# Attention phase: each pair's substitution starts ten operations earlier, and its result is stored ahead of the masked product

## What is computed

```
P = where(strict, (k*beta) @ k.T * L, 0)          # per head and chunk, 64 x 64
Ainv = inverse by powers of P;  v = Ainv @ v;  k_cumdecay = Ainv @ (k*beta*exp(g))
step over chunks:  attn = where(tril, q @ k.T * L, 0);  v_new = v_i - kcd_i @ S
                   o_i = (q*exp(g)) @ S + attn @ v_new
                   S   = S*exp(g_last) + (k*exp(g_last-g)).T @ v_new
o = rmsnorm(o) * silu(gate);   x = x + o @ Wo
```

## Time and profile before

| what | value |
|---|---|
| median of 3 runs | 1290.39 us (1282.06 to 1291.25) |
| profiled execution | 1290.93 us, span 1288.8 us |
| TensorE busy over the span | 1040.7 us (81%) |
| VectorE busy over the span | 937.1 us (73%) |
| ScalarE busy over the span | 605.8 us (47%) |
| GpSimd busy over the span | 399.1 us (31%) |
| substitution, L1772 and L1769 | 416 + 416 operations, 152.4 + 149.6 us busy on VectorE |
| product with the inverse, L1422 | 2048 matmuls, 101.7 us busy, 69.2 us of waits before them |
| first and last substitution in the trace | 265 and 855 us from the span's start |

### The profile page before, as it was taken

One profiled execution on the slowest core, in us unless ns is written; L12 is line 12 of the kernel. 1 busy time (PEld: TensorE's weight loads), 2 busy tenths in 40 slices (PEclk: granted clock), 3 DMA queues, 4 the chain that ended last, 5 costly groups with the idle time before them and its releaser, 6 DMA issues. The chain is left out here.

```text
span 1288.8 us, 38550 instructions
## 1 busy us (share of the span) xinstructions
PE 1040.7 (81%) x15510; PEld 757.8 (59%) x15510; DVE 937.1 (73%) x2432; ACT 605.8 (47%) x1614; POOL 399.1 (31%) x580
## 2 busy tenths in 40 slices
PE   3999977766887877887878786567999979699968
PEld 2888844434555554555555555445888867245546
DVE  3877645378777888877887877752777638699966
ACT  2343254434666666665666754455433245110134
POOL 3666520210211211211211211112666538520027
PEclk9999988977988889988988987776999979799969
DMA  9000022334334344334334334310000004866003
GB/s 259 1 1 1 1 100 75 87 75 100 66 90 97 82 77 100 70 86 99 80 78 102 84 74 85 76 36 6 1 1 1 1 21 98 204 160 187 2 3 129
DMA packets 282626, 93.32 MB, mean 72 GB/s; under 512 B 208976, under 2 KB 275408, under 8 KB 282448
## 3 DMA queue, kind: packets, MB, share of 16 engines
q1 hardware_dynamic: 247056, 84.03, 27.4%
q10 hardware_dynamic: 35392, 6.82, 2.8%
HBM read 56.20 MB, written 30.41 MB: 67 GB/s over the span
## 5 line engine op out<-in xcount | busy, mean ns | idle before, releaser
L1772 DVE TENSOR_TENSOR delta_tmp<-delta_PR 128x130 f32<-128x130 f32 (+12 forms) x416 | 152.4, 366 | 11.3
L1769 DVE TENSOR_TENSOR delta_PR<-delta_PR,delta_tmp 128x130 f32<-128x130 f32 (+12 forms) x416 | 149.6, 360 | 11.9
L1422 PE MATMUL psum<-delta_T,delta_pad 128*32 128x128 f32 x2048 | 101.7, 381 | 69.2 <-DMA delta_T<-inverse_scratch 68.6
L1422 PEld LDWEIGHTS psum<-delta_T,delta_pad 128*32 128x32 f32 x2048 | 86.2, 157 | 82.7 <-DMA delta_T<-inverse_scratch 75.5
L1873 POOL TENSOR_TENSOR delta_E<-delta_S,both_egl 128x128 f32<-128x128 f32 x32 | 13.5, 423 | 352.8 <-PE psum L1406 337.1
L1621 ACT ACTIVATE delta_y<-psum 32x128 f32<-32x128 f32 x256 | 68.5, 267 | 89.2 <-PE psum L1456 44.7
L506 POOL TENSOR_TENSOR ffn_H<-ffn_hid,ffn_H 128x512 fp32r<-128x512 f32 x48 | 61.6, 1289 | 59.2 <-DVE ffn_H L472 59.2
L1637 ACT ACTIVATE delta_wide<-delta_S 32x128 f32<-32x128 f32 x256 | 78.2, 306 | 3.2
L506 POOL TENSOR_TENSOR first_H<-first_hid,first_H 128x512 fp32r<-128x512 f32 x48 | 61.6, 1290 | 53.3 <-DVE first_H L472 53.3
L1469 PEld LDWEIGHTS psum<-delta_y,delta_Kd 32*32 32x32 f32 x2048 | 23.6, 113 | 91.5 <-ACT delta_y L1621 90.0
L1406 PE MATMUL psum<-delta_MV,delta_KT 32*32 32x128 f32 x2048 | 66.4, 280 | 10.6 <-ACT delta_E L1571 10.6
(11 more groups left out here) (278 smaller groups left out, 2587.0 us busy)
## 6 DMA issues: line engine op xcount, KB each, us to landing
within_scratch<-delta_PT SPq DMA_DIRECT2D x128, 64.0 KB, 2.1
delta_PR<-within_scratch SPq DMA_DIRECT2D x16, 512.0 KB, 4.3
inverse_scratch<-delta_PR SPq DMA_DIRECT2D x16, 512.0 KB, 3.1
space_T<-taps_scratch SPq DMA_DIRECT2D x8, 1024.0 KB, 6.1
X<-taps_scratch SPq DMA_DIRECT2D x8, 1024.0 KB, 9.0
X<-in_x SPq DMA_DIRECT2D x32, 128.0 KB, 10.1
turned_scratch<-gates_XT SPq DMA_DIRECT2D x16, 256.0 KB, 2.3
delta_xT<-turned_scratch SPq DMA_DIRECT2D x32, 128.0 KB, 3.8
```

What stands on the lines that cost most here:

```text
L1422: i = pe.matmul(bank[3][SUB * c:SUB * c + SUB, (2 * w + g) * P:(2 * w + g + 1) * P], M.pad[:, from_c:from_c + SUB], M.T[t % 2][:, h * P:(h ...
L1769: i = v.tensor_tensor(after, after, t3, ALU.add)
L1772: i = v.tensor_tensor(t3, column.to_broadcast([P, j, n_after]), row.to_broadcast([P, j, n_after]), ALU.mult)
```

## The change

`SOLVE_AHEAD = 10` is added, and `solve` counts its 29 turns of a slot ten operations further on: turns 0 to 28 of an even slot now are operations 10 to 38 of the pair (before 0 to 28), turns 0 to 18 of the odd slot are operations 39 to 57, and turns 19 to 28 of the odd slot are operations 0 to 9 of the next pair. On SyncE `pair_back` moves ahead of `within_out`. No instruction is added or removed.

```diff
+SOLVE_AHEAD = 10
...
         at(keys_out, n - 2)
         at(keys_in, n - 3)
+        if n % 2 and 0 <= (n - 5) // 2 < NT // 2:
+            pair_back((n - 5) // 2)
         at(within_out, n - LAG_FORM)
-        if n % 2 == 0:
-            if 0 <= (n - 2) // 2 < NT // 2:
-                pair_in((n - 2) // 2)
-            if 0 <= n - 5 < NT:
-                inverse_in(e, B, M, S, n - 5, (0, 1), S.i_diag)
-        elif 0 <= (n - 5) // 2 < NT // 2:
-            pair_back((n - 5) // 2)
+        if n % 2 == 0 and 0 <= (n - 2) // 2 < NT // 2:
+            pair_in((n - 2) // 2)
+        if 0 <= n - 5 < NT:
             inverse_in(e, B, M, S, n - 5, (0, 1), S.i_diag)
...
     def solve(n, first, end):
-        m = (n - 4) // 2
-        if not 0 <= m < NT // 2:
-            return
-        R = M.PR[m % 2]
-        R3 = R.rearrange("p (c i) -> p c i", i=SUB)
-        for k in range(first, end):
-            k += HALF_SOLVE if n % 2 else 0
+        for turn in range(first, end):
+            m, k = divmod((n - 4) * HALF_SOLVE + turn + SOLVE_AHEAD, 2 * HALF_SOLVE)
+            if not 0 <= m < NT // 2:
+                continue
+            R = M.PR[m % 2]
+            R3 = R.rearrange("p (c i) -> p c i", i=SUB)
             if k == 0:
```

## The result

| | median of 6 | lowest to highest |
|---|---|---|
| before | 1289.74 us | 1282.06 to 1293.81 |
| changed | 1273.39 us | 1266.43 to 1277.10 |

A forecast was written before the change was run, and what follows sets the result against it. No engine was full: a transfer chain from PT set odd slots, VectorE, after waiting for delta_rs, even ones. Even slots 7.3, pair 14 1.2, tail 4.5, less 0.3, gave 12.7 us off 1290.93: 1278 us, range 1260 to 1293.

The forecast's parts named there:

- part 4: Odd slot, next pair started early: its read lands 1.8 us before needed, cost 0; only the very first pair costs 0.3 us.
- pair 14's 1.2: Even slot of pair 14: the wait shows on delta_Bm, 2.55 us; gain 1.2 us.
- Part 1: Pair's write goes out early in the odd slot, so delta_y and delta_rs in the even slot no longer wait for it.
- Part 2: Even slots: VectorE gets heavier operations, 1.3 us growth each; 24.2 us of waits less 13 x 1.3 leaves 7.3 us gained.
- Part 3: Odd slots: VectorE loses 1.3 us of work, but their length hangs on the transfers from PT; counted as 0.
- Part 5: SyncE's order: the write waits ahead of PT's four transfers and the even tile's delta_T loads go earlier; cost and gain 0.
- Part 6: The end: the last pair's first eleven operations move into a slot where VectorE idles, 4.5 us; pair 14 gains 1.2.
- B: Rival, chance 0.14: VectorE's relief in odd slots shortens the pair of slots, so the growth is not paid; 17 us more, 1261.
- C: Rival, chance 0.17: the small net gain per even slot (0.5 us) is eaten, only the tail stays; 1287 us.
- D: Rival, chance 0.07: ScalarE's own loads keep its wait, so even slots pay 1.3 us for nothing; slower, 1307 us.
- E: Rival, chance 0.05: the odd slot's TensorE product runs at full clock, 1.4 us for each of 13 slots; 1260 us.

The follow-up runs named there:

- the repeat: The unaltered change (SOLVE_AHEAD = 10 and the early write) measured again on another chip against the kernel before: 1274.75 us, ratio 0.9924.
- first experiment: The change with SOLVE_AHEAD = 0, so only the pair's write moves ahead of PT's four transfers: 1259.78 us, ratio 0.9806 to the kernel before.
- second experiment: The change with SyncE's old order, so only the lead of ten stays: 1287.72 us, ratio 1.0008 to the kernel before.
- third experiment: The change plus the odd tile's delta_T loads issued ahead of PT's four transfers: 1213.71 us, ratio 0.9437 to the kernel before.
- lead of twenty: The third experiment's kernel with SOLVE_AHEAD = 20 in place of 10: 1244.13 us, ratio 0.9689 to the kernel before.

## Why the prediction was right, point by point

From the start of PT at 308.77 to the one at 808.90 before (13 odd and 13 even slots, the same ones 307.82 to 795.71 after), summed by the starts of PT:

| stretch | before | after | measured | forecast |
|---|---|---|---|---|
| up to that first PT | 308.8 | 307.8 | -0.9 | -1.3 |
| 13 odd slots | 242.9 | 240.8 | -2.1 | 0 |
| 13 even slots | 257.2 | 247.1 | -10.1 | -6.9 |
| the rest | 479.9 | 475.8 | -4.1 | -4.5 |

(The forecast of the sum's first part is split here by slots: one even slot with its 2.89 us wait lies in the first row, with the 0.3 of part 4; pair 14's 1.2 in the third.)

The forecast had also split its chances by a line at 1277.5 us, 0.43 for faster and 0.50 for no change; the first measurement (0.9875) lies on the less likely side, the repeat (0.9924) on the other. The time was right, and which side of that line the change falls is not settled.

*Part 1, the early write:* right. 11.5 us after PT against 11.7; nobody waits for it. The first experiment shows that the place on SyncE's list is the whole of the gain, and the second that the lead without it is worth nothing. That goes further than the forecast, which took both for one step. What held the write in the kernel before was mostly the issuing of the four transfers, and less their wait for PT. The pair was solved when PT started at 637.29, the four were issued from 638.06 on, and that alone took SyncE 2.97 us:

```profile
638.06 2.97 SPq L1339 DMA_DIRECT2D within_scratch<-delta_PT  x4
641.07 0.49 SPq L1333 DMA_DIRECT2D inverse_scratch<-delta_PR  x1
```

*Part 2, VectorE pays:* right, and the price a little high. It was 1.3 us in the slot compared under the first experiment and 1.05 on average; VectorE's busy time in an even slot grew from 15.34 to 16.42 us, 1.1. delta_QK comes at 7.9 us against 8.0. The term for the even slots came out 3.2 us too small: the slot that I had worked from and the one at 598.61 gave what the difference said (19.72 to 19.00, for 2.03 - 1.3; 20.48 to 18.99, for 2.79 - 1.3), while others gave more, most of all the one at 406.11 (20.08 to 19.49, where 0.6 more was forecast). There VectorE had also waited 1.87 us ahead of delta_Bm, before the substitution, and after the change only 0.99; my sum took the start of the substitution as fixed. So the 3.2 us are in part the price and in part that start.

*Part 3, the odd slot gives nothing back:* right. 18.69 us on average before, 18.52 after; the wait for delta_o_sq took the difference. (The second experiment's odd slots, 18.20 on average, show that they move by a few tenths without a known cause.) The third experiment shows the chain that I had named, by cutting it.

*Part 4, the cover:* right. 1.8 us were estimated, and the lead of twenty, which asks for the pair ten operations earlier, waits every time.

*Part 5:* right; TensorE waits for delta_gate, 28.5 us in all at its weight loads, and in the even slots VectorE has no wait for it behind delta_QK.

*Part 6, the tail:* right, 4.1 against 4.5. From the last PT to the last addition to x it was 83.0 us before and 78.9 after. With the early write alone it was 82.4, with the lead alone 81.0: most of it comes only with the lead, as forecast.

*The rivals.* B was not awake: with the transfers' chain in place the growth is paid. Without that chain the odd slots do give it back (14.98 us with the lead, 15.81 without), as B would have it. C, 1287, lies above both measurements and their intervals; its working has a slip, for 13 x 0.5 added to 1278 give 1285, and 1287 needs the whole 7.3 us and pair 14's 1.2. D fell with the result itself: delta_y no longer waits for the write, although its own loads stand where they stood. E stayed away as argued: the odd product still ran at 0.50 of the clock behind its wait. When the third experiment took the wait, the clock rose to 1.00 and the product fell from 3.59 to 1.96 us, as in the earlier trace rows. The Trainium skill ("TensorE: Matmul & The Clock Gate", Part 1) has the throttled clock as the default and activity as what releases it, and the trace agrees with that. What the clock alone contributed to those 60 us no run separates.

## What to carry to other kernels

Look first at what stands ahead of a late transfer on its own issuing queue. Here 41.8 us of waits hung on a write that was ready and queued behind four transfers, of whose 3.8 us 0.8 were their wait and 3.0 the issuing itself; 64 us more hung on loads queued behind the same four and behind a read that waited for their landing; moving issue instructions cost nothing that shows, while moving operations to make room cost about 1.1 us in every second slot. And a gain that is found in one half of a two-slot period is only worth its difference if the other half hangs on something else: find that chain, and test the shift again after it is cut, since the sign of its worth can turn (1% lost before; about 0.5% won after, by kernels measured on two chips).

## What was not expected

TensorE's product in even slots also got faster, though nothing was done to it. Before, TensorE had waited 1.96 us for delta_y, 1.1 us ahead of it, and its granted clock was 0.55 during the product's weight loads (2.96 us from 647.13). After, it was busy without a gap in the 3.67 us ahead, the clock stayed at 1.00, and the loads take 1.69 us:

```profile
637.17 1.69 PEld L1421 LDWEIGHTS psum<-delta_T,delta_pad 128*32 128x32 f32 x64 [0.17 <-issue]
```

Over the kernel the product's matmuls fell from 101.7 to 90.5 us busy. By my reading it bought no time here, because VectorE ended the even slot.
